# Layer 0 of a two-layer conditioned sequence network: scores before the first output, scale and shift by ScalarE

## The reference

```
xn = layer_norm(x); q, k, v = xn @ Wq + bq, xn @ Wk + bk, xn @ Wv + bv
layer 0 (16 heads of 32): att = softmax over keys of (q k' + mask term); y = att v
layer 1 (8 heads of 64):  q = softmax over a head's features, k = softmax over positions; y = q (k' v)
scale, shift = split(silu(cond) @ W_emb + b_emb)          # one row a sequence
h = layer_norm(y) * (1 + scale) + shift
x = x + silu(h) @ W_out + b_out
```

## Time and profile before

| | us |
|---|---|
| median of 3 runs (lowest, highest) | 1071.45 (1070.84, 1073.52) |
| the profiled execution, its own time | 1071.39 |
| its span, first to last instruction | 1069.4 |
| PE busy | 1026.1 |
| DVE busy | 772.6 |
| ACT busy | 610.6 |
| POOL busy | 589.3 |
| mean granted clock of TensorE | 0.995 |

### The profile page before, as it was taken

How to read it: one execution, slowest core, us unless ns; L and a number is a source line. 1 busy time by engine, 2 the same in 40 slices (tenths; PEclk the granted TensorE clock), 3 DMA queues, 4 the chain that set the end, 5 groups by cost and what they waited for, 6 DMA issues and landing times. The chain is left out here.

```text
span 1069.4 us, 26077 instructions
## 1 busy us (share of the span) xinstructions
PE 1026.1 (96%) x8558; PEld 890.8 (83%) x8558; DVE 772.6 (72%) x1344; ACT 610.6 (57%) x2021; POOL 589.3 (55%) x874
## 2 busy tenths in 40 slices
PE   6999999999999999999998799999999999999997
PEld 5768888988888888988887688888888888888886
DVE  6656766676667766677679587877888777877875
ACT  5356667766687666876697354344444444444434
POOL 3454456544655446554566476655655565666631
PEclk9999999999999999999999899999999999999999
DMA  9624110111112110221213212222211111111101
GB/s 307 230 82 144 44 63 25 64 62 43 41 44 64 51 52 24 64 64 43 63 51 115 79 46 65 65 66 64 64 43 51 53 64 54 54 64 64 44 21 59
DMA packets 46117, 73.72 MB, mean 69 GB/s; under 512 B 8274, under 2 KB 14546, under 8 KB 46068
## 3 DMA queue, kind: packets, MB, share of 16 engines
q1 hardware_dynamic: 46064, 73.11, 21.2%
q10 hardware_dynamic: 4, 0.00, 0.0%
HBM read 56.28 MB, written 16.81 MB: 68 GB/s over the span
## 5 line engine op out<-in xcount | busy, mean ns | idle before, releaser
L482 POOL TENSOR_SCALAR stat<-stat 128x1 f32<-128x1 f32 x128 | 35.7, 279 | 352.4 <-DVE stat L939 325.3
L1337 PE MATMUL bank<-xt_hi,w_hi 128*128 128x256 f32 x752 | 214.0, 285 | 1.5 <-DVE xt_lo L963 1.5
L1338 PE MATMUL bank<-xt_lo,w_hi 128*128 128x256 f32 x752 | 209.1, 278 | 0.0
L1339 PE MATMUL bank<-xt_hi,w_lo 128*128 128x256 f32 x752 | 209.0, 278 | 0.0
L671 ACT ACTIVATE prob<-prob,neg_max 128x128 f32<-128x128 f32 x512 | 198.9, 397 | 7.2 <-DVE neg_max L977 7.2
L1337 PE MATMUL bank<-w_hi,xt_hi 128*128 128x512 f32 x384 | 157.4, 410 | 0.0
L1339 PE MATMUL bank<-w_hi,xt_lo 128*128 128x512 f32 x384 | 151.3, 394 | 0.0
L1338 PE MATMUL bank<-w_lo,xt_hi 128*128 128x512 f32 x384 | 150.4, 392 | 0.0
L1337 PEld LDWEIGHTS bank<-xt_hi,w_hi 128*128 128x128 f32 x752 | 141.9, 189 | 4.8 <-issue 1.9
L1338 PEld LDWEIGHTS bank<-xt_lo,w_hi 128*128 128x128 f32 x752 | 142.2, 189 | 1.2
L1339 PEld LDWEIGHTS bank<-xt_hi,w_lo 128*128 128x128 f32 x752 | 141.8, 189 | 0.0
(11 more groups left out here) (126 smaller groups left out, 2373.2 us busy)
## 6 DMA issues: line engine op xcount, KB each, us to landing
x_in<-in_x_dram SPq DMA_DIRECT2D x32, 256.0 KB, 2.7
x_res<-in_x_dram SPq DMA_DIRECT2D x32, 256.0 KB, 3.0
between_layers<-x_res SPq DMA_DIRECT2D x32, 256.0 KB, 2.0
x_in<-between_layers SPq DMA_DIRECT2D x32, 256.0 KB, 3.2
x_res<-between_layers SPq DMA_DIRECT2D x28, 256.0 KB, 2.6
out_dram<-x_res SPq DMA_DIRECT2D x28, 256.0 KB, 2.0
room<-in_L_cond_W_emb_dram SPq DMA_DIRECT2D x8, 512.0 KB, 7.0
prob<-in_L_cond_emb_w_dram SPq DMA_DIRECT2D x4, 512.0 KB, 8.6
```

The source lines that it names most:

```text
L482: pool.tensor_scalar(v[:, 8:9], v[:, 7:8], EPS, None, ALU.add).then_inc(s[a_in].sem, 1)
L1337: pe.matmul(o, a_hi, b_hi, start=start, stop=False)
L1338: pe.matmul(o, a_hi, b_lo, start=False, stop=False)
L1339: return pe.matmul(o, a_lo, b_hi, start=False, stop=stop)
```

## The change

Layer 0 gets another order at the border between two steps, and its scale and shift go from VectorE and GpSimd to ScalarE. In the diff the parts of every engine that matter stand; the same edits are made in `step_mixed`, and `film_scale`, `add_shift` and their semaphore `z_a_full` are gone. BEGIN and MIXED keep the banks that the start and the mixed step had.

```diff
-        FIRST = dict(X=(0, 1), PT=(4, 5), Q=(6, 7), K=(0, 1), V=(3, 4), PV=(7, 7), Y=(2, 2), H=(6, 7), O=(5, 6))
+        FIRST = dict(X=(5, 4), PT=(4, 5), Q=(6, 7), K=(0, 1), V=(3, 6), PV=(7, 7), Y=(2, 2), H=(6, 7), O=(5, 6))
-        MIXED = FIRST | dict(K=(6, 7), V=(0, 1), Q=(3, 4))
+        MIXED = FIRST | dict(X=(0, 1), K=(6, 7), V=(0, 1), Q=(3, 4))
+        BEGIN = FIRST | dict(X=(0, 1), V=(3, 4))
...
             def step0(i, n, f, k, late, slot):          # SyncE
                 load_front(1 if i == G - 2 else 0, n)
+                if late:
+                    store(0, late + (-1), 0)
                 load_back(0, k, 0)
...
-                store(0, k, 0)
...
             def step0(i, n, f, k, late, slot):          # GpSimd
...
-                if i == 0:
-                    pool.wait_ge(film_dve, 3)
-                add_shift(k, 0)
...
-                add_shift(k, 1)
...
-            def film1(k, b, bk=SECOND):                 # ScalarE
-                at = k + (b - B)
+            def film(l, k, b, bk=SECOND):
+                at = k + (b - B * l)
                 act.wait_ge(*done(s["h_pe"], k + b))
                 act.wait_ge(*done(s["s_full"], k + (b - 2)))
                 for c in range(C):
-                    scale, shift = (film_ab[:, 1, i, c, at.const:at.const + 1] if at.reg is None
-                                    else film_ab[:, 1, i, c, bass.ds(at.value(), 1)] for i in range(2))
+                    scale, shift = (film_ab[:, l, i, c, at.const:at.const + 1] if at.reg is None
+                                    else film_ab[:, l, i, c, bass.ds(at.value(), 1)] for i in range(2))
...
             def step0(i, n, f, k, late, slot):          # ScalarE
+                exps(k, 0, (0, 1))
                 if late:
+                    film(0, late + (-1), 1, FIRST)
                     tanh(late + (-1), 1)
-                exps(k, 0, (0,))
+                exps(k, 0, (2,))
                 if late:
                     s_high(late + (-1), 1)
-                exps(k, 0, (1,))
                 if i == 0:
                     act.wait_ge(w_split[0][WO], 1)
                 q_out(f, slot, 0)
-                prob_turned(k, 0, (0,))
-                exps(k, 0, (2,))
-                prob_turned(k, 0, (1,))
                 exps(k, 0, (3,))
+                prob_turned(k, 0, (0, 1))
                 q_out(f, slot, 1)
...
+                if i == 0:
+                    act.wait_ge(film_dve, 3)
+                film(0, k, 0, FIRST)
                 y_t_out(k, 1)
...
             def step0(i, n, f, k, late, slot):          # VectorE
-                if late:
-                    film_scale(late + (-1), 1)
                 softmax(k, 0, (0, 1))
                 if i == 0:
                     film(0, 5)
                 if late:
-                    silu(late + (-1), 1)
+                    output(FIRST, late + (-1), 0)
                 softmax(k, 0, (2,))
                 if late:
+                    silu(late + (-1), 1)
+                softmax(k, 0, (3,))
+                if late:
                     s_low_part(late + (-1), 1)
-                softmax(k, 0, (3,))
...
-                film_scale(k, 0)
+                if i == 0:
+                    film(1, 2)
...
                 v_add(0, FIRST, f, slot, 1)
...
-                output(FIRST, k, 0)
-                if i == 0:
-                    film(1, 6)
...
             def turn_yn(l, k, b, bk=SECOND):            # TensorE
                 to = (FIRST, bk)[l]["H"][b]
-                claim(to, (s["z_full" if l else "z_a_full"], k + b))
+                claim(to, (s["z_full"], k + b))
...
             def step0(i, n, f, k, late, slot):          # TensorE
                 scores(k, 1 - slot, 0)
+                if late:
+                    output(0, FIRST, late + (-1), 0)
+                    turn_yn(0, late + (-1), 1)
                 queries0(f, slot, 0)
...
                 turn_yn(0, k, 0)
+                if i == 0:
+                    film(1, 2)
                 weigh(k, 1 - slot, 1)
...
                 y_rows(k, 1)
                 values(0, FIRST, f, slot, 1)
                 if i == 0:
                     need(0, WO)
-                output(0, FIRST, k, 0)
-                turn_yn(0, k, 1)
-                if i == 0:
-                    kept = before[6]
-                    film(1, 6)
-                    claim(6, *kept)
...
             def step1(i, n, f, k, late, slot):          # ScalarE
                 kt_out(k, 0)
                 if i == G:
+                    film(0, late + (-1), 1, FIRST)
                     tanh(late + (-1), 1)
                 qt_out(k, 0)
...
             def step1(i, n, f, k, late, slot):          # VectorE
                 if i == G:
-                    film_scale(late + (-1), 1)
                     silu(late + (-1), 1)
```

More of the change, by code:

```diff
@@ L840, in step1 @@
                     act.wait_ge(film_dve, 6)
-                film1(k, 0)
+                film(1, k, 0)
                 tanh(k, 0)
@@ L863, in drain @@
                 qt_out(f, 0, DRAIN)
-                film1(k, 0, LATER)
+                film(1, k, 0, LATER)
                 tanh(k, 0)
@@ L867, in drain @@
                 s_high(k, 0)
-                film1(k, 1, LATER)
+                film(1, k, 1, LATER)
                 tanh(k, 1)
@@ L871, in drain @@
                 for b in range(GROUP):
-                    film1(f, b, DRAIN)
+                    film(1, f, b, DRAIN)
                     tanh(f, b)
@@ L1006, in y_norm @@
                 moments(1, b, y_s[:], "stats2", "aggr2", k + b)
[L1008 to L1012, removed]
             def silu(k, b):
@@ L1118, in start @@
                 dve.wait_ge(par_in[0], PARS[0])
-                v_add(0, FIRST, f, 0, 0)
+                v_add(0, BEGIN, f, 0, 0)
                 cut_mask(1)
-                v_add(0, FIRST, f, 0, 1)
+                v_add(0, BEGIN, f, 0, 1)
                 for b in range(GROUP):
-                    xt_low(pair(1), 1, b)
+                    xt_low(pair(1), 1, b, BEGIN)
                 embed_sum(0, 0, 5)
             def step0(i, n, f, k, late, slot):
-                if late:
-                    film_scale(late + (-1), 1)
                 softmax(k, 0, (0, 1))
@@ L1327, in film, with turn @@
                 last.then_inc(film_pe, 1)
-            def turn(n, b):
-                claim(FIRST["X"][b], (s["xt_low"], n + b))
+            def turn(n, b, bk):
+                claim(bk["X"][b], (s["xt_low"], n + b))
                 pe.wait_ge(*done(s["xn_full"], n + b))
                 for c in range(C):
-                    last = pe.transpose(bank[FIRST["X"][b]][:, c * P:(c + 1) * P], xn[:, b, c * P:(c + 1) * P], ident[:])
+                    last = pe.transpose(bank[bk["X"][b]][:, c * P:(c + 1) * P], xn[:, b, c * P:(c + 1) * P], ident[:])
                 last.then_inc(s["xn_turned"].sem, 1)
@@ L1511, in start @@
                 for b in range(GROUP):
-                    turn(f, b)
+                    turn(f, b, BEGIN)
                 first_queries(f)
@@ L1527, in start @@
                 need(0, WV)
-                values(0, FIRST, f, 0, 0)
-                values(0, FIRST, f, 0, 1)
+                values(0, BEGIN, f, 0, 0)
+                values(0, BEGIN, f, 0, 1)
                 for b in range(GROUP):
-                    turn(pair(1), b)
+                    turn(pair(1), b, BEGIN)
                 embed(0, range(KE), 5, EMB_SUMS[0])
@@ L1590, in step_mixed @@
                 weigh(k, 1 - slot, 1)
-                turn(n, 0)
-                turn(n, 1)
+                turn(n, 0, MIXED)
+                turn(n, 1, MIXED)
                 y_rows(k, 1)
@@ L1624, in step1 @@
                 turn_yn(1, k, 1)
-                turn(n, 0)
-                turn(n, 1)
+                turn(n, 0, SECOND)
+                turn(n, 1, SECOND)
             def drain(k, f):
```

69 lines of the change are left out of this document (32 added, 37 removed).

## The result

The changed kernel takes 1074.24 us (median of 20 runs, 1073.15 to 1076.06), the kernel before 1070.97 on the same chip (20 runs, 1068.62 to 1076.31). The ratio is 1.0027 with an interval of 1.0016 to 1.0038: slower by 0.2 to 0.4%, with its middle inside the 0.3% that the forecast called no change, but only just. The forecast was a difference of +0.1 us; the medians differ by 3.3. The profiled executions are 1071.39 us before and 1073.47 after.

What follows compares the result with a forecast made beforehand. PE bounds the kernel before; after the change a closed ScalarE and VectorE chain bounds regular steps. From 1071.39 us: -3.49 + 13 x 0.19 (2.5) + 0.3 + 0.83 = +0.1, forecast 1071.5, own range 1069 to 1074.

Steps and rivals of the forecast that it cites:

- B: Rival: handing over film in regular steps is dearer, step 0.27 us longer still (0.46 in all), 1075.0 us; chance 0.2.
- The old wait: Regular step of layer 0: PE's wait of `output` for `s_low` goes, gaining 0.90 us.
- The wait for `y_t`: Regular step: `y_rows` waits for ScalarE's `y_t_out` behind film, a new PE wait of 0.44 us.
- The wait for bank 7: Regular step: `queries0` half 1 waits for ScalarE's film of sequence 1, a new wait of 0.72 to 0.82 us.
- the closed chain: Regular steps: a ScalarE and VectorE loop from film to film replaces PE as bound; a step becomes 0.19 us longer.
- Rival A: Bank 7 wait hidden because exps or VectorE run ahead: step 0.52 us shorter, 1061.5 us; chance 0.15.
- the sixth: Regular step after half 1 of `queries0`: PE's order and what others bring stay as before; step 0.19 us longer in sums.
- Step 0: First step: `scores` of sequence 1 comes 3.49 us earlier, through waits gone and no slow clock.
- The clock: Step 0: slow 1.2 GHz stretch goes because PE is nowhere idle; 0.85 given that full clock stays, otherwise 1.6 us return.
- rival C: Clock falls in step 0 all the same: 1073.1 us, inside the no-change bound; chance 0.1.
- The end of layer 0: Step 14 and mixed step: film before the same bank costs between nothing and 1.51 us, placed at 0.3.
- The first step of layer 1: PE's wait for ScalarE's copy `qt_out`, queued behind tanh, comes 0.83 us later because film precedes tanh.

Runs made afterwards that it cites:

- order_only: Kernel after, but layer 0's scale and shift again by VectorE and GpSimd (new order and banks kept); 1059.97 us, ratio 0.9884.
- both: Kernel after with the edits of bank4 and split together; 1059.93 us, ratio 0.9885.
- film_only: Kernel before with ScalarE's film in layer 0, old order of PE's work and old banks; 1071.16 us, ratio 0.9997.
- bank4: Kernel after with the turned y of sequence 1 of the step before in bank 4 instead of bank 7; 1064.16 us, ratio 0.9923.
- split: Kernel after with one chunk of `values(f,1)` ahead of the `y_rows` that waits; 1075.06 us, ratio 1.003.
- longer: Kernel after with one more 512-column addition on VectorE per regular step, between `xt_low` and `v_add`, result unused; 1083.3 us, ratio 1.0101.
- both_w2: The kernel both with two waits that wait for nothing ahead of `queries0` in PE's queue; 1059.9 us.
- both_early: The kernel both, with ScalarE's film and tanh of layer 0's last sequence ahead of the last query exponentials in the mixed step; 1058.6 us, ratio 0.9869.
- both_w1: The kernel both with one wait that waits for nothing ahead of `queries0` in PE's queue; 1060.0 us.
- both_w5: The kernel both with five waits that wait for nothing ahead of `queries0` in PE's queue; 1059.36 us.
- shifted: Kernel before with one wait that waits for nothing ahead of `queries0` in PE's queue; 1073.3 us in its one run.

## Why the prediction came out as it did

**What came true, and by what luck.** The time stayed inside no change, by a hair, and the two waits are where the prediction put them. But by its own signs the prediction is wrong on the step: it named 34.4 and more as the sign of B and 0.25 us a step as the point from which B decides, and the step is 34.43, 0.38 longer over the thirteen. That the time held all the same is in part luck: 1.0 us that no one forecast came back in layer 1, and step 0 kept the full clock in the profiled execution, which most executions of the new order did not.

**The old wait.** Gone, as forecast, and 0.90 us is about what it cost, but only 0.53 shows in order_only. Two things took the rest. There `output` starts 0.24 us later behind `scores` than in the kernel after (1.34 for 1.10), for want of `xt_low`. And 693 distances of matmuls are at the slower rate where the kernel before has 186: 507 x 4.5 ns is 0.19 a step. The same rate (688 of 1116) explains nearly all of the difference between both, 33.34, and the old order without its wait, 34.03 - 0.90 = 33.13.

**The wait for `y_t`.** Forecast 0.44. `y_rows` starts 2.90 us behind `turn_yn` where it took 2.47, so 0.43 late, in the kernel after as in film_only. Taking it away gives 0.34 (bank4 against both). Right in place and size. It doesn't count in the kernel after, as split shows.

**The wait for bank 7, and the closed chain.** Right, and the placing was close: from `turn_yn` to the first `softmax` part 7.98 us (313.26 to 321.24), which is what the placing had (314.67 to 322.65). PE went on 0.05 us behind the film (327.33 to 327.38), the cheaper of the two that were left open. From `turn_yn` to half 1 the twelve steps have 14.09 us on average, where the placing had 328.76 - 314.67 = 14.09. Rival A, the hidden wait at 33.5 us a step, is what order_only does and not this change: its step is 34.43. Rival B has the right size, 34.4, but by another cause: the second film starts right behind the exponentials, at 325.85, and PE 0.05 behind its end. "A closed chain of ScalarE and VectorE" leaves out the link in which the miss then came, PE's own.

**The step that failed** is the sixth: "From there on the order on PE, and what the others must bring, is as before." I added 0.19 us to the old step and took the stretch from half 1 of `queries0` to the next `turn_yn` at its old length. It is 0.19 us longer on average of the twelve steps, 0.21 in the pair shown. There, from half 1 to `scores(k,1)` it takes 3.81 us (292.94 to 296.75) where the kernel before has 3.69, from 294.56 to this row of its timeline:

```profile
298.25 1.17 PE L1408 MATMUL bank<-room,q_t 32*128 32x128 f32 x32
```

Of the 0.12 some 0.11 is the first matmul behind the wait, which the next follows at 0.222 us, and the rest slower matmuls. From `scores(k,1)` to `turn_yn(k,0)` it takes 16.51 (296.75 to 313.26) where it took 16.42 (298.25 to 314.67); there half 0 of `keys` runs at 117.8 ns in every step, not in every other. The averages are 3.84 for 3.70 and 16.52 for 16.47. So of the 0.19 us some 0.11 is the restart behind the new wait, which the prediction put at nothing, and some 0.07 the slower rate. The step grew by 0.39, forecast 0.19.

**Step 0.** From `turn_yn(k,0)` to `scores` of step 1 it takes 7.53 us (forecast 7.50), and from there to `scores` of sequence 1 11.69 (forecast 11.54). That one is at 90.15 where the kernel before has 93.77: -3.62 for the forecast -3.49. But 0.31 of it was there ahead of `turn_yn` (70.93 for 71.24), so the change gave 3.31. The placing was close; the terms listed beside the 3.49 are not its sum (0.90 + 1.59 + 1.6 - 0.19 = 3.90), since the list leaves out the wait for bank 7 in step 1.

```profile
70.93 0.65 PE L1435 MATMUL bank<-ident,yn 128*128 128x128 f32 x4 [1.38 <-DVE spare L908]
...
78.46 1.17 PE L1394 MATMUL bank<-room,q_t 32*128 32x128 f32 x32
...
90.15 1.17 PE L1394 MATMUL bank<-room,q_t 32*128 32x128 f32 x32
```

The clock is the part that this execution hides. I gave 0.85 that it stays, since PE is nowhere idle in the stretch. It isn't, and yet of the ten profiled executions with the new order only three (after, longer, both_w2) keep 1.00 in step 0. In five (order_only, bank4, split, both, both_early) it is 0.50 for 3.4 us, and in two (both_w1, both_w5) for 6.8, from 1.4 to 2.8 us behind the same wait of 1.38 us. The first row below is of both_w2, then come split and both_w1:

```profile
70.99:78.54 7.55, 7.55 (x77) 6.46 (x77) 3.28 (x8) 4.12 (x9) 0.29 (x2) 1.00 0.78 267
```

```profile
73.60:77.00 3.40, 3.40 (x34) 2.92 (x23) 1.26 (x4) 2.05 (x4) 0.00 (x0) 0.50 0.88 329
```

```profile
71.36:78.19 6.83, 6.83 (x54) 5.89 (x54) 1.47 (x4) 3.38 (x7) 0.00 (x0) 0.50 0.65 226
```

From `turn_yn(k,0)` to `scores` of step 1 the three take 7.52 to 7.55 us, the five 9.08 to 9.14 and the two 10.69 and 10.72. So a stretch of 3.4 us costs 1.6, as forecast, but rival C is the usual case and not the one in ten. (In split `scores` of sequence 1 is 1.85 later, at 92.00; the rest of that is its longer wait for bank 7.) With the old order the clock is low in step 0 for 3.4 us in before and film_only and for 6.8 in shifted.

Of the 20 runs of the kernel after, the 8 with a mean clock of 0.995 average 1073.7 us, the 6 with 0.992 average 1074.9. This is probably a part of why the median lies 0.8 us above the profiled execution.

**The end of layer 0.** `scores` of sequence 1 of the last regular step is 1.28 us late against before (-3.62 and 13 steps that grew by 4.90), that of the mixed step 2.25. So step 14 to mixed cost 0.97, forecast 0.3: an under-sized term, inside its bounds of 0 to 1.51. The first step of layer 1 waits for ScalarE at 615.07 where the kernel before has 612.02: 3.05 late, so 0.8 more, forecast 0.83. The film does stand between the copy and tanh as placed:

```profile
611.89 0.58 ACT L718 ACTIVATE prob<-bank 128x512 f32<-128x512 f32 x1
612.37 1.50 ACT L686 ACTIVATE z_s<-bank,film_ab 128x128 f32<-128x128 f32 x4
613.90 0.63 ACT L694 ACTIVATE th<-z_s 128x512 f32<-128x512 f32 x1
```

**Sum.** -3.62 + 4.90 + 0.97 + 0.80 = +3.05, with the 0.31 in it that was there ahead of the change; 1.0 of it came back in layer 1, so the profiled executions differ by 2.08. Of the 1.0, 0.4 is PE's wait for `spare` (0.9 to 0.5). I haven't traced the rest. Against the forecast's +0.1 the large terms are 2.4 from thirteen steps and 0.7 from the mixed step, less the 1.0.

By the rule of the Trainium skill (ScalarE: Activation LUTs, What ACT_TABLE_LOAD costs) one such ACTIVATE takes 186 + 2 x 93 + 0.833 x 128 = 479 ns, and the next starts 93 ns before its end. For four that is an estimate of 1.54 us to the next start and 1.64 to their end; the 1.49 and 1.58 of the prediction are a slip, and by the rule the step would be 0.29 longer, not 0.18. The trace again does not agree: 1.39 and 1.51 us here (314.04 to 315.43, and the row of the film).

## What to carry to other kernels

Two edits that are each neutral or good can close a chain through a shared bank: before you give a bank to a slower reader, look who next claims it, and whether that one can have another bank. Test whether a wait is worth removing by asking what takes its place: if the critical part is a loop over several engines, taking a wait beside it away gains nothing (split), and adding to a link costs in full (longer). A prediction by small joints over many steps should carry a term for the restart behind each new wait and for the engine's own rate. Here 0.19 us a step in "as before" is 2.4 of the 2.9 us by which the kernel up to layer 1 went over the forecast. And a single profiled execution should not decide whether a clock falls: look at every trace that has the stretch.

## What the runs showed of the hardware

- Two rates of the same matmul: 113.3 and 117.8 ns for 256 columns, constant over a block of 24, at a granted clock of 1.00. The pattern can repeat every two steps, and the same instructions of a loop can change between the two from turn to turn (film_only, both). A single wait more in the queue changed the pattern in one kernel (shifted, +0.10 us a step) and one, two or five did not in another. Its cause is open.
- Behind an idle time of 0.4 to 0.5 us the first matmul's successor comes at 0.222 us instead of 0.113.
- Whether the clock falls to 1.2 GHz behind 1.38 us of idle time in step 0 differs between executions of the new order, though PE is never idle behind it: three of ten kept 2.4 GHz, five had 1.2 GHz for 3.4 us (1.6 us more until `scores`) and two for 6.8 us (3.2 more).
